# A two-layer macaron block on one core: warm-up, the first normalized groups and the shared experts' parts are placed elsewhere in a hand-written order

## What is computed

```python
x = x + 0.5 * moe(layernorm(x), ...)
x = x + attention(layernorm(x), ...)
x = x + 0.5 * moe(layernorm(x), ...)

def moe(x):
    scores = softmax(x @ gate_w)
    topk_w, topk_idx = top_k(scores, 2)
    routed = sum over the two chosen experts of topk_w * (silu(x @ w_gate) * (x @ w_up)) @ w_down
    shared = silu(x @ sw_gate) * (x @ sw_up) @ sw_down
    return routed + shared
```

## Time and profile before

| | us |
|---|---|
| median of 3 runs | 907.17 |
| lowest and highest of them | 905.27, 909.38 |
| the profiled execution | 902.63 |
| its span, first to last instruction | 900.8 |
| mean granted TensorE clock in it, full speed = 1 | 0.994 |

### The profile page before, as it was taken

How to read it: one execution, slowest core, us unless ns; L and a number is a source line. 1 busy time by engine, 2 the same in 40 slices (tenths; PEclk the granted TensorE clock), 3 DMA queues, 4 the chain that set the end, 5 groups by cost and what they waited for, 6 DMA issues and landing times.

```text
span 900.8 us, 18966 instructions
## 1 busy us (share of the span) xinstructions
PE 874.1 (97%) x5779; PEld 784.6 (87%) x5779; DVE 673.9 (75%) x2359; ACT 553.0 (61%) x1605; POOL 392.4 (44%) x534
## 2 busy tenths in 40 slices
PE   9999999999998999999999999999999998999997
PEld 4778898888887899998999988999999996889996
DVE  6787669588897897776787767878587675757786
ACT  6765555467665767766667675667467674435562
POOL 0577787200002343342243343555258684316672
PEclk9999999999999999999999999999899999999999
DMA  9256984640000110000000005993001044524474
GB/s 347 95 167 241 358 311 146 133 85 12 1 1 1 36 36 25 24 1 1 2 1 1 1 1 152 317 304 89 1 1 48 25 162 155 228 73 135 134 250 169
DMA packets 52449, 96.23 MB, mean 107 GB/s; under 512 B 5824, under 2 KB 37184, under 8 KB 50304
## 3 DMA queue, kind: packets, MB, share of 16 engines
q1 hardware_dynamic: 44672, 73.20, 25.2%
q0 software_dynamic: 7680, 21.83, 7.7%
HBM read 44.99 MB, written 50.02 MB: 105 GB/s over the span
## 4 chain that ended last, share of the span: by engine, by line
PE 89%; DVE 6%; ACT 3%; issue 2%; POOL 0%; DVEq 0%; ACTq 0%; POOLq 0%
PE ps L825 43%; PE ps L830 37%; PE ps L1086 4%; PE ps L991 2%; PE ps L962 2%; DVE RR L1350 1%; PE ps L868 1%; ACT RR L1129 1%; ACT SP L1319 1%; DVE PA L1745 1%; DVE RA L1350 0%; POOL SP L1911 0%; DVE X L1638 0%; DVE SP L1784 0%; DVE X L1350 0%
## 5 line engine op out<-in xcount | busy, mean ns | idle before, releaser
L1911 POOL TENSOR_SCALAR SP<-SP,RC 128x128 f32<-128x128 f32 (+1 forms) x256 | 192.4, 768 | 252.0 <-DVE RC L1794 251.8
L1350 DVE TENSOR_TENSOR RR<-ps,RR 128x256 fp32r<-128x256 f32 (+2 forms) x322 | 157.7, 525 | 73.6 <-ACT RR L1129 72.5
L830 PE MATMUL ps<-RR,RA 128*128 (+1 forms) x894 | 162.8, 319 | 8.1 <-DVE RA L1350 4.8
L1129 ACT ACTIVATE RR<-ps 128x256 fp32r<-128x256 f32 (+2 forms) x322 | 137.3, 469 | 29.8 <-PE ps L825 27.7
L1319 ACT ACTIVATE SP<-SP,NB 128x128 f32<-128x128 f32 (+1 forms) x256 | 113.5, 444 | 66.9 <-DVE NB L1784 66.6
L830 PEld LDWEIGHTS ps<-RR,RA 128*128 128x128 f32 x894 | 129.7, 189 | 14.2 <-issue 13.2
L825 PE MATMUL ps<-xh,RR 128*128 128x512 f32 x368 | 133.6, 407 | 0.3 <-DVE PA L1350 0.3
L830 PE MATMUL ps<-RR 128*128 128x256 f32 x768 | 103.9, 285 | 3.0 <-DVE RR L1350 3.0
L1745 DVE SCALAR_TENSOR_TENSOR PA<-R,IW,PA 128x128 f32<-128x128 f32 x240 | 84.6, 414 | 29.6 <-ACT R L1311 29.4
L1879 POOL DMA_INDIRECT yr<-FA,IDX x78 | 84.3, 1081 | 47.5 <-DVE FA L1672 17.8
L830 PEld LDWEIGHTS ps<-RR 128*128 128x128 f32 x768 | 97.1, 192 | 4.0 <-DVE RR L1350 3.6
(11 more groups left out here) (252 smaller groups left out, 1886.2 us busy)
## 6 DMA issues: line engine op xcount, KB each, us to landing
xg<-stage SPq DMA_DIRECT2D x15, 1161.0 KB, 14.5
FA<-xg SPq DMA_DIRECT2D x78, 129.0 KB, 2.9
kept<-RR SPq DMA_DIRECT2D x8, 1216.0 KB, 6.0
RR<-kept SPq DMA_DIRECT2D x8, 1216.0 KB, 12.4
X<-yr POOLq DMA_DIRECT2D x6, 512.0 KB, 5.4
RAW<-yr SPq DMA_DIRECT2D x6, 512.0 KB, 5.3
RAW<-wex_in SPq DMA_DIRECT2D x8, 352.0 KB, 8.1
RAW<-wsh_in SPq DMA_DIRECT2D x6, 384.0 KB, 7.4
```

The source lines that it names most:

```text
L830: return e.matmul(o, a, c, start=start, stop=stop, skip_group_check=True)
L1129: return e.activation(o, i, ACT.Copy)
L1350: return e.tensor_tensor(o, p, q, alu)
L1911: ins = e.tensor_scalar(SP[:, k, i, o:o + w], SP[:, k, i, o:o + w], RC[:, k, 2 * i + z:2 * i + z + 1], None, ALU.mult)
```

## The change

It moves stages in `order()`, splits two kinds of them, and needs a few waits changed for that.

- Head: 30 warm-up matmuls instead of 40. Group 0 is centred and flipped ahead of group 1, its four rows shared by DVE and ACT; the low half of the first shared weight is made after the flips. Both `unturn` of a batch go to one bank, and one DVE step (`untwist`) adds both. They stand between the two halves of `gu` (0,0,0). Groups 3 and 2 are centred by DVE and ACT half each, one `down` earlier in the PE's queue than their flips.
- The X addition is a stage of its own (`deposit`), placed some operations later on the DVE.
- First sparse loop: the first two `turn_x` stand ahead of the last two `down`, the last two `lift` one tile later, and `gu` of group 2, thirds 0 and 1, stand in the loop's last two tiles. The row numbers of POOL (`index`) are a stage of their own. A `tag` is one POOL operation instead of two.
- Four shared parts of MoE 1 have `gu` split into a gate half (`gu`) and an up half (`gv`), six matmuls each (`APART` also names the first of MoE 0). Parts 0 and 1 of MoE 1 go between the last units of the attention, parts 1 to 3 and `down` 0 around the last group's normalization. `down` 1 and `gu` 4 now stand ahead of `count`, `tables` and `offs` one step behind `gu` 5.
- Second sparse loop: `turn_x` 0 stands ahead of the last `down`, `turn_x` 1 behind it; `gu` of group 3, third 0, stands in the loop's tail.

```diff
+APART = ((0, 0, 0), (1, 0, 0), (1, 0, 1), (1, 1, 0))
...
-    yield from [("warm", 40), ("tokens",)]
+    yield from [("warm", 30), ("tokens",)]
...
-    yield from high(("sh", 0, 0)) + [("moments", "m0", 0, 8, 0)] + centre("m0", 1, 4, "dve") + centre("m0", 0, 0, "act")
-    yield from low(("sh", 0, 0)) + [("flip", "m0", 1, 4, 5), ("flip", "m0", 0, 6, 7)] + high(("sh", 0, 1))
+    yield from high(("sh", 0, 0)) + [("moments", "m0", 0, 8, 0)] + centre("m0", 0, 0, "dve", "act") + centre("m0", 1, 4, "dve")
+    yield from [("flip", "m0", 0, 4, 5), ("flip", "m0", 1, 6, 7)] + low(("sh", 0, 0)) + high(("sh", 0, 1))
...
-    yield from low(*parts[11:14]) + part_of("down", 8) + lifts(*parts[10:14]) + prefetch(0)
+    yield from [("turn_x", 0, 0), ("turn_x", 0, 1)] + part_of("down", 7) + low(*parts[11:14]) + lifts(*parts[10:14])
+    yield from part_of("down", 8) + [("deposit", 0, 3)] + prefetch(0)
...
-            yield from low(*parts[14:16]) + lifts(*parts[14:16])
+            yield from low(*parts[14:16])
+        if j == 1:
+            yield from lifts(*parts[14:16])
...
+        elif j == 38:
+            yield ("gu", 0, 2, 0)
+        elif j == 39:
+            yield from [("gu", 0, 2, 1), ("tm", 0, 2, 0)]
...
-    yield from [("wo", 61), ("pv", 62), ("flip_p", 63), ("wo", 62), ("pv", 63), ("wo", 63)]
+    yield from task_of("gu", 0) + [("wo", 61), ("pv", 62), ("flip_p", 63)] + task_of("gv", 0) + task_of("tm", 0)
+    yield from [("wo", 62), ("pv", 63)] + task_of("gu", 1) + task_of("gh", 0) + task_of("gl", 0) + [("wo", 63)]
     yield ("second",)
...
+    yield from task_of("gv", 1) + [("stats", "m1", 12, 4, 12)] + task_of("gu", 2) + task_of("tm", 1)
+    yield from [("rough", "m1", 12, 4, 12), ("moments", "m1", 12, 4, 12)] + task_of("gh", 1) + task_of("down", 0)
+    yield from centre("m1", 3, 12, "dve", "act") + task_of("gu", 3) + [("flip", "m1", 3, 6, 7)] + task_of("gv", 3)
+    yield from task_of("tm", 2) + task_of("gl", 1) + [("logits", 1, 3, 6)] + task_of("tm", 3)
+    yield from task_of("gh", 2) + task_of("gl", 2) + [("pick", 1, 2), ("sel", 1, 2)] + task_of("gh", 3) + task_of("down", 1)
+    yield from task_of("gu", 4) + [("shift", 1, 2), ("raise", 1, 2), ("count", 1, 2, 7), ("place", 1, 2, 7), ("choose", 1, 2)]
+    yield from marks(1, 3) + scatters(1, 3) + task_of("tm", 4) + task_of("gl", 3) + task_of("gh", 4) + task_of("down", 2)
+    yield ("deposit", 1, 0)
+    for k in range(5, 9):
+        yield from task_of("gu", k) + task_of("tm", k) + task_of("gl", k - 1) + task_of("gh", k)
+        if k == 5:
             yield ("tables", 1)
+        yield from task_of("down", k - 2)
+        if k == 5:
+            yield ("offs", 1, 6)
+        elif k == 7:
+            yield ("deposit", 1, 1)
+    yield from task_of("gl", 8) + prefetch(1) + task_of("down", 7) + [("turn_x", 1, 0), ("index", 1, 0)]
+    yield from task_of("down", 8) + [("turn_x", 1, 1), ("index", 1, 1), ("deposit", 1, 2)]
...
+        elif j == 38:
+            yield ("gu", 1, 3, 0)
         elif j == 39:
-            yield ("store", 0, 0)
+            yield from [("store", 0, 0), ("tm", 1, 3, 0)]
...
-                    for z in range(2):
+                    for z in {"gu": (0,), "gv": (1,)}[kind] if a in APART else range(2):
...
-                    then(e.tensor_copy(rows[:, :, D], W2[:, 1, 4 * g:4 * g + 4]))
-                    then(e.tensor_scalar(rows[:, :, D + 1], token[:, 4 * g:4 * g + 4], float(T), None, ALU.add))
+                    then(e.tensor_copy(rows[:, :, D:DW], TAGS[:, 1, 4 * g:4 * g + 4, :]))
```

More of the change, by code:

```diff
@@ L98, in sparse @@
             if j + 2 < NT:
-                yield ("turn_x", n, j + 2)
+                yield from [("turn_x", n, j + 2), ("index", n, j + 2)]
             yield from fills(j)
@@ L128, in order @@
[L128 to L132, removed]
@@ new lines, in order @@
+    yield from [("unturn", 0, 0, 1), ("unturn", 0, 1, 1), ("untwist", 0, 0, 1), ("pick", 0, 0), ("gv", 0, 0, 0)]
+    yield from part_of("gu", 1) + part_of("tm", 0) + [("sel", 0, 0), ("shift", 0, 0)] + part_of("gu", 2) + [("squares", 2)]
+    yield from part_of("tm", 1) + [("raise", 0, 0), ("stats", "m0", 14, 2, 14)]
+    yield from [("count", 0, 0, 6), ("place", 0, 0, 6), ("choose", 0, 0)] + marks(0, 0, 1) + scatters(0, 0, 1)
+    yield from [("root", 1, 8, 8)] + part_of("down", 0) + part_of("gu", 3) + [("moments", "m0", 8, 8, 8)]
@@ new lines, in order @@
+    yield from part_of("tm", 2) + centre("m0", 3, 12, "dve", "act") + centre("m0", 2, 8, "dve", "act")
+    yield from part_of("down", 1) + [("flip", "m0", 3, 6, 7)] + part_of("tm", 3) + high(parts[0])
+    yield from part_of("down", 2) + [("flip", "m0", 2, 6, 7), ("logits", 0, 3, 1)] + low(parts[0]) + high(parts[1])
+    yield from [("deposit", 0, 0), ("logits", 0, 2, 3)] + high(parts[2])
+    yield from [("unturn", 0, 3, 6), ("unturn", 0, 2, 6), ("untwist", 0, 1, 6)]
+    yield from high(parts[3]) + part_of("gu", 4) + [("pick", 0, 1)] + part_of("down", 3) + [("sel", 0, 1), ("shift", 0, 1)]
@@ new lines, in order @@
+    yield from part_of("tm", 4) + [("raise", 0, 1), ("count", 0, 1, 6), ("place", 0, 1, 6), ("choose", 0, 1)] + marks(0, 2, 3)
+    yield from spread(0, 2, 0) + spread(0, 3, 0) + [("tag", 0, 2)] + spread(0, 2, 1) + [("index", 0, 0), ("index", 0, 1)]
+    yield from [("tag", 0, 3)] + spread(0, 3, 1) + high(*parts[4:6]) + part_of("gu", 5) + [("tables", 0), ("tail", 0)]
+    yield from part_of("tm", 5) + part_of("down", 4) + high(*parts[6:9]) + low(*parts[1:3]) + part_of("gu", 6) + [("offs", 0, 7)]
@@ new lines, in order @@
+    yield from low(parts[3]) + part_of("tm", 6) + part_of("down", 5) + [("deposit", 0, 1)] + high(*parts[9:12]) + low(parts[4])
+    yield from part_of("gu", 7) + low(*parts[5:7]) + part_of("tm", 7) + part_of("down", 6) + high(*parts[12:16])
+    yield from low(*parts[7:9]) + part_of("gu", 8) + low(*parts[9:11]) + lifts(*parts[8:10]) + part_of("tm", 8)
+    yield from [("turn_x", 0, 0), ("turn_x", 0, 1)] + part_of("down", 7) + low(*parts[11:14]) + lifts(*parts[10:14])
+    yield from part_of("down", 8) + [("deposit", 0, 3)] + prefetch(0)
@@ L381, in between4 @@
[L381 to L390, removed]
@@ L417, in fill6 @@
             yield from [("sum", 1, 3, 0), ("sum", 1, 3, 1)]
-    yield from shared(1, [3], fill6)
+    yield from (st for st in shared(1, [3], fill6, 1) if st != ("tm", 1, 3, 0))
     yield from [("store", 3, 0), ("store", 3, 1)]
@@ L498, in tally @@
             n["read", st[3]] = (n["read", st[3]] or ()) + ((st[4], n["xn", st[4]]),)
-        if kind == "down" and st[3] == 2 or kind == "sum":
-            n["xres"] += 2 if kind == "down" else 1
-            if kind == "down":
+        if kind in ("deposit", "sum"):
+            n["xres"] += 2 if kind == "deposit" else 1
+            if kind == "deposit":
                 n["emptied", 4], n["emptied", 5] = n["xres"] - 1, n["xres"]
@@ L770, in macaron_kernel @@
         GU = [st for st in stages if st[0] == "gu"]
+        UP = [("gv", *st[1:]) if st[1:] in APART else st for st in GU]
         TURNS = {}
```

91 lines of the change are left out of this document (48 added, 43 removed).

## The result

| | before | changed | ratio, 95% interval |
|---|---|---|---|
| median of 20 runs each, us | 907.88 | 904.93 | 0.9968 (0.9957 to 0.998) |
| the profiled execution | 902.63 | 904.25 | |
| its span | 900.8 | 902.5 | |
| mean granted clock in it | 0.994 | 0.992 | |

The change saves 3.0 us, 0.3%. Forecast were 6.5 (907.17 to 900.7), a clear gain; it is within the half per cent that I had called no change. The median is 4.2 us above the forecast, outside the forecast's own range (897 to 904) and inside the wider one of 8 in 10 (894.5 to 905.5).

The account below looks back on a forecast made before the run. The PE, busy 97% of the span, was taken as the bound, leaving idle time and low clock to win. Savings of 2.4 + 2.1 + 3.0 - 1.0 = 6.5 us from 907.2 gave 900.7, range 897 to 904 (8 in 10: 894.5 to 905.5).

Parts of the forecast that it names:

- the clock: Low-clock stretches: 1.7 us regained at the first loop's end, 1.7 lost behind the `offs` wait (bounds 0 to 3.4).
- the end of the first loop: Last tile's `sink` wait of 1.72 goes, 1.7 of clock regained, 0.4 of new wait left: 3.0 us saved.
- 0.3 + 0.4 + 1.36: Waits said to go: routing's drained bank 0.3, a normalized group 0.4, the first tile's low half 1.36 us.
- 0.8 + 1.3: First loop: second tile's gated-rows wait, 0.98 less 0.2 left; last `sink` wait, 1.72 less 0.4 of new wait.
- Head and start of the first loop: Shorter warm-up and filled waits save 2.4 us in the head, 2.1 at the loop's start.
- the waits of 1.36 and 0.98: First loop's start: first tile's low half (1.36) and second tile's gated rows (0.98, 0.2 left); 2.1 us saved.
- 4.5 above that execution: Median of the runs shown, 907.2 us, against the profiled execution; cause unknown, so the saving was subtracted from the median.
- the DVE's multiply is ahead of it: End of first loop: a DVE multiply (0.69) delays the normalization, leaving only 0.4 us of new wait.
- rival (b): Early gains given back in the first loop as fetched rows or result slots come no earlier: 905.2 us; chance 0.18.
- a sign of being wrong as a whole: First loop showing waits on fetched rows, or more than one low-clock stretch that no wait precedes.
- Attention's end: Attention's end and second layer's shared parts: 5.9 us of waits gone, 5.2 new (`offs` 3.1), 1.7 of clock: 1.0 lost.
- End of the kernel: One third's `gu` moved into the second loop's last tiles: nothing taken; bounds 0.4 us saved, 1.3 lost.
- Rival (c): Low clock answers to unbroken load, so removing rests brings more such stretches, about 3.4 us each; 910.9 us; chance 0.04.

Follow-up runs that it names:

- a3: Changed kernel with the end of the first expert loop put back as before; 898.96 us, 0.998 of the kernel before.
- (a): Runs of one chip: changed kernel, unedited, against the kernel before; clock-free time (span times granted clock) 892.8 against 897.6 us.
- (c): Runs of another chip: changed kernel, unedited, against the kernel before; clock-free time 893.4 against 897.5 us.
- (e): Runs of a chip with the stall: changed kernel, unedited, against the kernel before; clock-free time 900.9 against 903.2 us.
- a2: Changed kernel with the head and the start of the first loop put back as before; 902.38 us, 1.0002 of the kernel before.
- a4: Changed kernel with the attention's last units and second layer's shared parts in the old order; 900.14 us, 0.9985 of the kernel before.
- a1: Changed kernel run again without edit; 900.30 us against 901.24 for the kernel before, 0.9988.
- b1: Changed kernel with the `offs` products one shared part later; 895.00 us against 901.64 for the kernel before, 0.9935.
- c1: b1 plus the DVE's and ACT's multiply of the attention's first group ahead of the last `sink`; 894.58 us, 0.9913 of the kernel before.
- e2: Changed kernel without edit, on a chip with the stall; 911.90 us, 1.0014 of the kernel before.
- c3: c1 plus the flip of the attention's first group behind the last `gu`; 893.90 us, 0.9909 of the kernel before.
- d1: c3 with the end of the second expert loop put back as before; 901.63 us against 909.68 for the kernel before, 0.9908.
- b3: b1 plus the flip of the attention's first group behind the last `gu`; 893.46 us, 0.9917 of the kernel before.

## Why the prediction was wrong

The size was wrong, and so was the call of a clear gain. Two steps failed. The first is the clock, which the sum took as even (1.7 gained at the end of the first loop, 1.7 lost at `offs`): it went against the change, by 0.7 to 4 us. The second is the end of the first loop: its new waits were put at 0.4 and are 2.6, and the 3.0 us booked there are 0.5 (a3). Segments, from the traces without the stall (b4 is the kernel before, c2 the changed one; half of each low stretch taken off):

| segment | before (b4) | changed (c2) | saved | forecast |
|---|---|---|---|---|
| start to first `gu` | 16.5 | 15.0 | 1.6 | 1.7 |
| to first `hidden` of loop 1 | 50.4 | 48.7 | 1.8 | 0.3 + 0.4 + 1.36 |
| to the attention's first index scores | 112.5 | 111.9 | 0.6 | 0.8 + 1.3 |
| to first `hidden` of loop 2 | 621.2 | 618.7 | 2.6 | 0.7 |
| to the end | 97.7 | 98.6 | -1.0 | 0 |

(Forecast is without its two terms for the clock, -1.7 and +1.7.) In sum 5.6 against 6.5; by the means of the runs 4.8 (a), 4.1 (c), 2.3 (e). The parts undone in a2 to a4 give 2.2 + 0.5 + 2.7 = 5.4; less the 0.9 of the kernel's end that is 4.5, beside the 4.8 of a1.

- **Head and start of the first loop: right up to the first `hidden` on a chip without the stall**, to 0.3 us each; the waits of 1.36 and 0.98 are gone in a1 and c2. But the 0.8 for the second of them was given back before the loop's end, and the runs of a2 give 2.2 for the 4.5 in all. With the stall it fails, and the trace that I had was one without. "4.5 above that execution, whose cause the profile cannot show": most likely it was the trace of one sort of chip beside the times of the other.
- **End of the first loop: wrong.** "I leave 0.4 of a new wait": it is 1.50 for the flip alone, 0.66 behind it, and 0.4 more than before for the X addition (1.2 for 0.8), 2.6 in all, more than the 1.72 that went; a3 still finds 0.5 of gain. The step that failed is "the DVE's multiply is ahead of it": I followed the DVE's queue and not ACT's, where the last `sink`'s copy stood ahead of the rows. Part of rival (b) happened too: a wait on fetched rows stands near 88 us in a1, a3, a4, b1, c1 and c2, with 0.5 to 1.3, where of the traces of before only b4 names one, of 0.30. Behind it a low clock of 3.4 us began in a3 (90.7) and c1 (89.8). I had named such waits as a sign of being wrong as a whole, and it came. In c2:

```profile
87.92 0.44 PE L981 MATMUL ps<-ident,FA 128*128 128x128 f32 x2 [0.54 <-DMA FA<-xg]
```

- **Attention's end: right in kind, undersized.** The new waits were put at 5.2 and are 4.2 in a1: `offs` 2.6 for 3.1 (my cover was also added wrongly: 0.3, two `down` and one `gu` are 6.4, not 6.3), `count` 0.4 for 0.7, around flip and `logits` 0.5 for 0.9, the second loop's first `turn_g` 0.4 for 0.5, and 0.2 for an X addition that I had not counted. So 1.7 instead of 0.7. The measured stretch gains more: from the transposes of unit 61 to the second loop's first `hidden` b4 takes 61.7 and c2 58.6, of which the PE idles 6.1 and 3.5. Half a us of these 3.1 no wait names, and the attention's middle (below) takes some of them back. The table load took 1.28 again, in the first trace of the changed kernel, and the next operation started 1.3 behind its start. That and an `offs` of 2.6 speak for the row, not for the 2.66 us of the Trainium skill (ScalarE: Activation LUTs, "What ACT_TABLE_LOAD costs"):

```profile
778.76 1.28 ACT L1242 ACT_TABLE_LOAD   x1
780.06 0.60 ACT L1242 ACTIVATE FA<-ps 128x512 f32<-128x512 f32 x1
```

- **End of the kernel**: 0.9 lost, inside its bounds of 0.4 saved and 1.3 lost.
- **The clock: the term that decides.** I set one stretch against another, 1.7 each, and got zero. The one that was to vanish stands in one of three traces of the kernel before; that it stood in the one I read was luck, and bad luck. The new one is real: three times in seven, at 1.7 or 3.4. In the mean of a1, c2 and e2 the changed kernel's clock is 0.0030 below that of before, nominally 2.7 us.

So of 2.3 to 4.8 us clock-free the clock takes 0.7 to 4 (1.4 to 3.9 and 0.5 to 3 when it is counted at 0.74). Ratios from 0.9971 to 0.998 lie in all four intervals (the first comparison, a1, c2, e2). Open is why the attention's middle, whose order is untouched, takes 0.8 us longer in the changed kernels (569.4 in a4 and c2 for 568.6 in b4). It isn't at one place: the delay grows by about 0.02 us with each unit (the same unit takes 8.247 us in a4 and c2 and 8.229 in b4), and no wait accounts for it.

Rival (c), more low stretches under unbroken load, named the right quantity; its cause finds no support, since taking the wait away raised the clock and adding it lowered it. It isn't ruled out for the rest: without the wait the clock still lies 0.0009 below that of the kernel before. What the PE does ahead of the recurring one at 640 us shows in c2 (timeline, then stretch):

```profile
631.95 1.85 PE L848 MATMUL ps<-gws,RT 128*128 128x16 f32 x16
633.66 1.93 PE L848 MATMUL ps<-gws,RR 128*128 128x16 f32 x16
...
635.00:640.00 5.00, 5.00 (x29) 4.71 (x29) 0.65 (x4) 0.77 (x2) 2.99 (x4) 0.69 0.00 0
```

The PE counts as busy, but for 3.6 us it runs 32 matmuls of 16 columns. Nine of the sixteen traces have a low clock that begins within 1.5 us of their end; the earlier trace rows is one. In seven, the same work has none. Sixteen of the kind, for the last group, also stand ahead of the low stretches near 764 to 774 us in a3, c2, c3 and d1. Those are four of the eleven traces with the new order there; none of the five with the old one has such a stretch, so this may be a second price of the change. With two such stretches in c2 the other sign came as well, more than one that no long wait precedes. So what stands ahead of these low clocks is a wait or such thin products, not full load. That thin products bring it about wasn't tried.

## What to carry to other kernels

Filling a wait moves the work behind it earlier, so follow the queues of every engine that feeds it, and ask which copy waits for the PE ahead of it: here ACT's. A long wait has two prices, its length and, in some executions, a low clock behind it; taking one of 2.6 us away brought 2.6 clock-free (b1 beside a1) and, in the mean of all runs, about 2 of clock. And read a single execution's low stretches as a draw, not as a property of the place.

The best versions here are c1, c3 and d1, at 0.991 of the time of before, three times the gain of the change; the runs don't tell them apart, nor from b3 (0.9917).

## What was not expected of the hardware

- Two sorts of chips, or of sessions: the same program takes 901 us on three and 908 to 910 on the others, where within the first 55 us the DVE pauses for 3 to 7 us, ACT for 4.5 or more and the PE for 0.3 to 4.3.
- Executions of one program differ in clock: 0.987 to 0.998 in the first twenty runs of the changed kernel, 907.1 to 900.3 us of span.
